# A sandwich layer on one core: couples of heads in the first 120 attention steps, VectorE's bias ahead of its split, and the projection one tile sooner

## The reference

```
x  = x + layernorm(attention(layernorm(x)))
x  = x + layernorm(ffn(layernorm(x)))

attention: xq = rms_norm(x @ wq.T), 32 heads of 64
           xk = rms_norm(x @ wk.T), xv = x @ wv.T, 8 heads of 64 (each serves 4 query heads)
           scores = xq @ xk.T / 8 + slope[h] * (key - query)
                    allowed only for 0 <= query - key <= 256
           out = softmax(scores) @ xv        -> [tokens, 2048]
           return out @ wo.T                 -> [tokens, 512]
```

## Time and profile before

| | us |
|---|---|
| median of three runs | 1213.42 |
| the profiled execution, its own time | 1213.68 |
| its span, first to last instruction | 1211.5 |
| PE busy | 1176.3 |
| DVE busy | 896.9 |
| ACT busy | 749.5 |
| POOL busy | 390.6 |

### The profile page before, as it was taken

The page is one execution under the profiler, slowest core; times in us unless marked ns, Lnnn a source line. Parts: engine busy times, 40 slices in busy tenths (PEclk is TensorE's granted clock), DMA queues, the critical chain, the costliest instruction groups (busy, mean ns, idle before and its releaser), DMA issues.

```text
span 1211.5 us, 26996 instructions
## 1 busy us (share of the span) xinstructions
PE 1176.3 (97%) x9016; PEld 998.2 (82%) x9016; DVE 896.9 (74%) x2388; ACT 749.5 (62%) x1641; POOL 390.6 (32%) x465
## 2 busy tenths in 40 slices
PE   7999999999999999999999999999999999999997
PEld 5878888887877778889898899889888888887876
DVE  5577778687999988888888888888865475546464
ACT  4645556555899888878888788888833343222230
POOL 3000000000689985544545454544421100202022
PEclk9999999999999999999999999999999999999999
DMA  5316355346567777445654556455555340302020
GB/s 174 104 44 232 151 200 216 127 196 252 194 227 238 230 240 239 145 164 167 219 177 152 174 185 214 142 166 168 160 195 173 121 129 35 104 1 88 18 70 36
DMA packets 99876, 189.89 MB, mean 157 GB/s; under 512 B 8096, under 2 KB 37920, under 8 KB 99744
## 3 DMA queue, kind: packets, MB, share of 16 engines
q1 hardware_dynamic: 99744, 188.21, 46.3%
HBM read 116.54 MB, written 71.63 MB: 155 GB/s over the span
## 4 chain that ended last, share of the span: by engine, by line
PE 85%; DVE 4%; ACT 3%; issue 3%; POOL 2%; DMA 2%; SPq 0%; POOLq 0%; ACTq 0%; DVEq 0%
PE bank L1330 21%; PE bank L1477 17%; PE bank L1404 13%; PE bank L1356 12%; PE bank L1367 11%; PE bank L1385 2%; PE bank L1383 2%; PE bank L1384 2%; PE bank L1393 2%; DMA z_in<-z_scr 1%; ACT pT_hi L866 1%; PE bank L1454 1%; POOL y_s L735 1%; PE bank L1298 1%; DVE y_s L989 1%
## 5 line engine op out<-in xcount | busy, mean ns | idle before, releaser
L859 ACT ACTIVATE p_sb<-u_sb,low 128x384 f32<-128x384 f32 (+2 forms) x512 | 274.6, 536 | 57.3 <-DVE low L1105 48.6
L1112 DVE TENSOR_TENSOR pT_lo<-bank,pT_hi 128x384 f16<-128x384 f32 (+2 forms) x512 | 232.4, 454 | 43.7 <-ACT pT_hi L866 32.9
L1356 PE MATMUL bank<-k_st,q_st 128*128 128x384 f32 (+2 forms) x1024 | 255.9, 331 | 2.4 <-DVE low L1105 2.4
L1105 DVE CUSTOM_DVE_ANT_0 u_sb<-bank,bias 128x384 f32<-128x384 f32 (+2 forms) x512 | 230.3, 450 | 34.2 <-PE bank L1356 18.6
L1367 PE MATMUL bank<-ident,p_sb 128*128 128x128 f32 x1152 | 217.9, 280 | 13.9 <-DVE pT_lo L1112 5.8
L866 ACT ACTIVATE pT_hi<-bank 128x384 f16<-128x384 f32 (+2 forms) x512 | 206.8, 404 | 38.9 <-PE bank L1367 34.1
L1356 PEld LDWEIGHTS bank<-k_st,q_st 128*128 128x128 f32 x1024 | 168.3, 192 | 17.6 <-DVE low L1105 2.7
L1367 PEld LDWEIGHTS bank<-ident,p_sb 128*128 128x128 f32 x1152 | 138.6, 140 | 49.4 <-ACT p_sb L859 22.3
L614 POOL TENSOR_TENSOR rstd<-var_eps,minus_half 128x1 f32<-128x1 f32 (+1 forms) x30 | 22.6, 754 | 426.0 <-DVE var_eps L971 426.0
L652 POOL TENSOR_TENSOR o_mid<-o_raw,inv_sum 128x256 f32<-128x256 f32 x128 | 80.9, 632 | 219.4 <-DVE inv_sum L1120 217.9
L1383 PE MATMUL bank<-v_st,pT_hi 128*128 128x65 f16 x1152 | 139.8, 193 | 0.5 <-DVE pT_lo L1112 0.5
(11 more groups left out here) (126 smaller groups left out, 2315.5 us busy)
## 6 DMA issues: line engine op xcount, KB each, us to landing
q_scr<-qk SPq DMA_DIRECT2D x64, 512.0 KB, 2.7
q_st<-q_scr SPq DMA_DIRECT2D x32, 1024.0 KB, 7.6
k_st<-k_scr SPq DMA_DIRECT2D x64, 256.0 KB, 3.2
o_scr<-o_out SPq DMA_DIRECT2D x128, 128.0 KB, 2.5
o_in<-o_scr SPq DMA_DIRECT2D x16, 1024.0 KB, 5.6
k_scr<-qk SPq DMA_DIRECT2D x16, 512.0 KB, 2.7
z_in<-z_scr SPq DMA_DIRECT2D x8, 1024.0 KB, 6.8
v_scr<-v_out SPq DMA_DIRECT2D x4, 1040.0 KB, 6.2
```

The lines of the kernel that those rows point to most:

```text
L859: nc.scalar.activation(p_sb[:, u % RING, 0:w], u_sb[:, u % RING, 0:w], ACT.Exp, scale=-1.0, bias=low[:, u % RING:u % RING + 1]).then_inc(p ...
L1105: nc.vector.tensor_tensor_reduce(out=u_sb[:, u % RING, 0:w], in0=bank[u % 2][:, 0:w], in1=bias[2 * u // UNITS][:, u % REP, at:at + w], sca ...
L1112: nc.vector.tensor_tensor(pT_lo[:, u % RING, 0:w], bank[2 + u % 2][:, 0:w], pT_hi[:, u % RING, 0:w], ALU.subtract).then_inc(pT_ready, 1)
L1356: mm = nc.tensor.matmul(bank[u % 2][:, 0:w], q_st[:, s, r, P * i:P * i + P], k_st[:, s, part, P * key:P * key + w], start=(part == 0), sto ...
```

## The change

1. **Couples.** For the first 120 units (`TWINS`) the stages behind the transpose are done for two neighbouring units at once: `round_pT` and `split_pT` are one ACT and one DVE instruction over two PSUM banks (2,3 or 6,7 in turn). The tables of lags have an entry for even and one for odd units. In a couple (A, A+1) PE transposes in steps A+2 and A+3, ACT rounds in step A+3, DVE splits in step A+5, PE weighs both in step A+6.
2. **VectorE's order.** In those steps DVE does `add_bias` of the step's unit first and the split of a couple second (`DVE_ORDER`).
3. **First scores ahead.** Scores, bias and exponential of units 0 and 1 stand ahead of the last product of the last `project`.
4. **LAG is 4 instead of 5.** The projection is woven in from tile of attention 4 on, and the tail projects tiles 12 to 15. The output weights are loaded and split in tiles 0 to 3 instead of 1 to 4. The loads of the attention outputs are cut in two, three quarters and the last quarter (`tile_last`).
5. **Smaller moves.** Five left-over query parts instead of four in a tile of attention; `sum_squares` of the keys of the first sequence goes behind product 21; the count of low bits is taken inside attention.

```diff
-LAG = TT + 1
+LAG = TT
-LAGS = {"split": 3, "scores": 0, "transpose": 2, "exps": 0, "weigh": 4, "take": 5, "invert_sums": 6}
-COUPLE_LAGS = {**LAGS, "take": 6, "invert_sums": 7}
+LAGS = {"split": (3, 3), "scores": (0, 0), "transpose": (2, 2), "round": (2, 2), "exps": (0, 0),
+        "weigh": (4, 5), "take": (6, 6), "invert_sums": (7, 7)}
+DVE_ORDER = ("transpose", "round", "exps", "weigh", "take", "scores", "split", "invert_sums")
+TWIN_LAGS = {**LAGS, "split": (5, 4), "round": (3, 2), "weigh": (6, 5), "invert_sums": (9, 9)}
+AHEAD = 2
+TWINS = LAG * UNITS - 2 * TT
...
-LATE_UNITS = (2, 4, 18, 20)
+LATE_UNITS = (2, 4, 18, 20, 22)
...
+def probability_bank(unit):
+    return unit % 2 + (6 if unit < TWINS and unit // 2 % 2 else 2)
...
             def round_pT(n, u):
+                A, w, at = UNITS * n + u, P * window(u // REP % TT)[1], u % RING
+                if A >= TWINS:
...
+                elif u % 2:
+                    act.wait_ge(pT_psum, A + 1)
+                    at_least(act, pv_done, A - RING + 1)
+                    nc.scalar.activation(pT_hi[:, at - 1:at + 1, 0:w], pairs[probability_bank(A) // 2][:, :, 0:w],
+                                         ACT.Copy).then_inc(pT_hi_ready, 2)
...
             def split_pT(n, u):
...
+                elif u % 2:
+                    dve.wait_ge(pT_hi_ready, A + 1)
+                    nc.vector.tensor_tensor(pT_lo[:, at - 1:at + 1, 0:w], pairs[probability_bank(A) // 2][:, :, 0:w],
+                                            pT_hi[:, at - 1:at + 1, 0:w], ALU.subtract).then_inc(pT_ready, 2)
...
             def unit_work(n, u):
-                for stage, nn, uu in due(n, u):
+                for stage, nn, uu in sorted(due(n, u), key=lambda d: UNITS * n + u < TWINS and DVE_ORDER.index(d[0])):
...
             def transpose_p(n, u):
-                at_least(pe, pT_ready, A - 1)
+                if A < TWINS:
+                    at_least(pe, pT_ready, A - A % 2 - 2)
+                else:
+                    at_least(pe, pT_ready, A - 1 if A > TWINS + 1 else TWINS - 2)
...
+                    if n == NGEMM - 1 and last:
+                        for u in range(AHEAD):
+                            scores(0, u)
...
-                    if n == QC + KVC:
+                    if n == QC + KVC + first:
                         sum_squares(b, 1)
```

More of the change, by code:

```diff
@@ L139, in due @@
 def due(n, u):
[L142 to L145, removed]
+    step = UNITS * n + u
+    for stage in LAGS:
+        for unit in range(max(0, step - LONGEST), min(step + 1, UNITS * B * TT)):
+            lag = (TWIN_LAGS if unit < TWINS else LAGS)[stage][unit % 2]
+            if stage in ("scores", "exps") and unit < AHEAD:
+                continue
+            if unit + lag == step and (stage not in OF_FOUR_HEADS or unit % REP == REP - 1):
+                yield stage, *divmod(unit, UNITS)
+def probability_bank(unit):
+    return unit % 2 + (6 if unit < TWINS and unit // 2 % 2 else 2)
 def transposed_at(n, u):
@@ L526, in attend @@
                 store_late(n, UNITS // 2, UNITS)
-                for i in range(TT // 2):
-                    store_o(n, 1, i)
+                if n == B * TT - 1:
+                    load_o(tile + 2)
+                store_o(n, 1, 0)
             sp.wait_ge(gemm_done, NGEMM * B)
@@ L534, in _ @@
                 attend(n)
-            for i in range(TT // 2, TT):
+            for i in range(1, TT):
                 store_o(B * TT - 1, 1, i)
+                if i < TT - 1:
+                    load_o(B * TT - LAG + i - 1, last=True)
             def load_z(tile, m, done):
@@ L888, in unit_work @@
                 for stage, nn, uu in due(n, u):
-                    work = {"transpose": round_pT, "exps": exps, "take": take_values}.get(stage)
+                    work = {"round": round_pT, "exps": exps, "take": take_values}.get(stage)
                     if work:
@@ L1075, in project @@
                             split_xT(b + 1)
+                        if n == NGEMM - 1 and last:
+                            for u in range(AHEAD):
+                                add_bias(0, u)
                         dve.wait_ge(v_hi_ready, TT * b + n - QC - KVC + 1)
@@ L1272, in _, with scores @@
             pe.wait_ge(const_ready, CONSTANTS)
+            def scores(n, u):
+                A, s, i, r = UNITS * n + u, 2 * u // UNITS, u // REP % TT, u % REP
+                key, tiles, _ = window(i)
+                w = P * tiles
+                if u % (UNITS // 2) == 0:
+                    pe.wait_ge(heads_loaded[s], 3 * DMA * (n + 1))
+                if n == 0 and u < 2:
+                    pe.wait_ge(v_ready, TT * (B - 1) + u + 1)
+                at_least(pe, u_ready, A - 1)
+                for part in range(2):
+                    mm = nc.tensor.matmul(bank[u % 2][:, 0:w], q_st[:, s, r, P * i:P * i + P],
+                                          k_st[:, s, part, P * key:P * key + w], start=(part == 0), stop=(part == 1))
+                mm.then_inc(s_psum, 1)
             def transpose_x(b):
@@ L1465, in _ @@
             lo_used = pe.value_load(lo_total[:].bitcast(mybir.dt.int32))
-            for t in range(B * TT - TT + 1, B * TT):
+            for t in range(B * TT - LAG + 2, B * TT):
                 finish_tile(t)
```

167 lines of the change are left out of this document (79 added, 88 removed).

## The result

The changed kernel takes 1249.05 us, the median of 4 runs (1245.67 to 1252.54). The kernel before, run beside it, took 1213.35 (1213.11 to 1215.61). The ratio is 1.029 [1.0259, 1.0321]: **slower by 35.7 us**. The prediction said 1245.5 and 1229 to 1263. The profiled execution took 1248.71 us with a span of 1246.5.

A forecast was written before the change was run, and what follows sets the result against it. PE bounds tiles with a projection; in the others PE, DVE, ACT and POOL are nearly full. From the profiled 1213.7 us, + 41.4 - 2 - 5.7 - 1.4 = 1246.0; predicted 1245.5 us, range 1229 to 1263.

The forecast's parts named there:

- loop, 120 units: Attention's first 120 units: scores, bias, couple's split, transpose, weighing, next odd scores form a slackless loop; +41.4 us, 35 to 47.
- clock in the loop: First 120 units: PE was taken to keep the full 2.4 GHz, so the sum held nothing for the clock.
- start of attention: First scores ahead, -2 us (0 to -4), and the `sum_squares` wait behind product 21 covered, -1.4 us.
- tile 4: Tile of attention 4 now carries a projection: 38.84 instead of 31.6 us, +7.2.
- tail: Output projection after attention: one tile less, -12.9 us.
- seven terms: Three-block loop: scores 0.44, hop 0.38, `add_bias` 0.56, split 0.97, hop 0.14, transposes 0.35, weighing 0.54; 3.38 us in all.
- The split over two banks: DVE's split of six blocks in the loop: 0.97 us, bounds 0.82 and 1.11, with no row showing one.
- The clock: Rival: in the loop PE's clock swings, at half clock for half of the 120 units; 27.6 us more, 1273 us; chance 0.08.
- First scores ahead: Start of attention: PE's idle time before the first scores and the half-clock stretch after it shrink; -2 us, 0 to -4.
- LAG: Tile 4 gains a projection, +7.2 us, and the tail loses a tile, -12.9 us; together -5.7 us.
- the rival of the tail's cover: Tail: late loads of the last outputs make PE wait up to some 5 us; 1250.5 us; 0.77 shared with the plain loop.
- The wait does not bind: Rival at PE's transpose (L1411): split done in time, POOL next at about 33 us a tile; 1204.5 us; chance 0.12.

The follow-up runs named there:

- kernel with full clock: Changed kernel with each odd unit's transposes in the first 120 units done three times over; 1242.87 us, ratio 1.0253 to the kernel before.
- the kernel with the sum in even steps: Changed kernel with an added VectorE sum of two SBUF operands behind each even unit's bias, 59 times in the first 120 steps; 1268.23 us.

## Why the prediction was right

It was right in direction, cause and size: 1249.05 measured, 1245.5 predicted, and most of its steps hold one by one. The sum ended 3.5 us low, 2.7 of it in the terms below: one that I had put at nothing was 6 us, and the loop, tile 4 and the tail, each 0.9 to 1.5 us shorter than foretold, hid more than half of that. That the total is so near is in part luck.

| term | predicted | measured | from |
|---|---|---|---|
| loop, 120 units | +41.4 | +39.9 | kernel with full clock: 171.1 less 131.2 for four tiles |
| clock in the loop | 0 | +6.1 | 46.0 less 39.9; the whole run says 6.2 |
| start of attention | -2 and -1.4 | -3.0 | of it the wait of the earlier trace rows -1.4 |
| tile 4 | +7.2 | +6.3 | 37.9 less 31.6 |
| tail | -12.9 | -14.4 | windows |
| tiles 5 to 15 | 0 | +0.1 | starts of `add_bias` |
| sum | +32.3 | +35.0 | span: +35.0 |

*The loop.* Its seven terms were each within 0.02 us but one: the bias. I counted its full duration (0.56); in the trace the split starts 0.48 after it, beside the one-column read. Over the eight turns of half a tile that is 8 x 0.08 = 0.64 us, about the 0.5 by which they came out shorter. The four tiles came out 1.5 us shorter than predicted. The split over two banks, for which I had kept 0.82 to 1.11, was 0.95 against 0.97. Signs foretold and seen: tiles of 42 to 46 us (43.3 to 45.3), DVE under 75% (28.7 / 43.3 = 66%), 60 waits of 1 us (54). The starts 3.4 apart were seen (3.3), but in 2 turns of 16 only. Tile 4, foretold at 38 to 39 us, took 37.9.

*The clock.* Here the step "In this trace it was granted the full 2.4 GHz in all tiles with short waits ... That speaks for full clock" failed. Those tiles had PE busy 30.0 of 32.6 us; nothing in them spoke for a tile in which PE is busy 27.8 of 43.3. Three times beside the one at the start the clock fell to 1.2 GHz, at 319, 408 and 452 us. Ahead of them PE was busy 3.8, 3.7 and 3.7 of 6.8 us; in the first two it was busy 6.2 of 6.8. PE is on the loop for about 1.3 of 3.29 us (scores, transposes, weighing), so a slower PE is paid at once. The Trainium skill, page "TensorE: Matmul & The Clock Gate", section "A second HAM failure mode: psum-queue depth-cycling", describes a clock that swings when PE idles briefly between groups of matmuls. By that rule the trace agrees, in part: one tile of four (336.8 to 380.1, clock 1.00) shows the same small gaps, in its like part with the same 3.7 us of PE in 6.8, and no fall. Why it was spared these rows don't tell. The sign that I had named for the clock, tiles over 48 us, could not have shown a cost of this size. I had given this rival 0.08 and 27.6 us, for half of the units; 6 us is what it took. A rival can be half true, and its price belongs into the sum by its chance or at least into the middle of the range.

*First scores ahead.* -2 predicted, -1.6 measured beyond the `sum_squares` wait. That one is gone as foretold: PE waits nowhere at L1350.

*LAG.* Tile and tail together: -8.1 instead of -5.7. The tail is shorter by one tile and by the 1.0 us of waits for `oT_lo`; no load stood bare, so the rival of the tail's cover did not come.

*The wait does not bind.* It does. But this rival was rightly built: with the loop opened, POOL was next as it said, at 34.8 us a tile where it said 33, and the kernel came to 1208.0 where it said 1204.5.

*What no run isolated.* Whether the order costs anything with single units, since every run without couples also had the split first. And what the 5.5 us between couples and singles are made of, both with the split first: the couples save 161 ns of DVE in a three-block couple (2 x 0.557 less 0.953), but they also have four banks instead of two and other lags.

## What to carry to other kernels

- Before moving one operation ahead of another on an engine, write down what each waits for and go round: if the second one's result is what the first one's producer stands behind, the two now alternate and nothing else matters. The sum of the terms round that loop, from rows of the trace, was right to 3% here.
- An order is not slow as such: couples with the split first took 1208.0 us, couples with the bias first and the split a step sooner 1210.0, and only bias first with the late split 1249.0. Move one step or one place in the order before dropping an edit, and look in the trace whether the run undid just what you meant: a condition on the number of units tied the order to the couples here.
- When a loop or wait goes, look for the engine that is next, and take load off it in the same step: with the split first, the kernel with POOL's fifth part gained 5 us on the one before, without it 11.

## What the runs showed of the hardware

**A slower PE by idling, a faster one by useless work.** The odd transposes done three times gave back 6.2 of 1249 us, and the runs agree to 1 us instead of 7. The clock read 0.99 over the four tiles instead of 0.88 to 1.00.

**A DVE sum of two SBUF operands stands still while POOL works.** In the kernel with the sum in even steps, 34 of 59 took 0.56 us on average. The other 25 began while POOL was in a tensor-tensor instruction (or within 0.06 us of its start) and took 1.34 on average, up to 2.88; in 23 of them the end came 0.41 us after POOL's instruction ended, as at 356.13 + 2.75 = 358.88 and 356.83 + 2.46 = 359.29. The bias and the split, each with one operand in PSUM, took 0.55 and 0.95 whatever POOL did. The Trainium skill, page "SBUF — State Buffer", section "SBUF: two separate sides", says that a VectorE operation with two SBUF inputs and a GpSimd operation that reads SBUF take turns whole, the one that starts first going first. The trace agrees. A probe meant to cost a known time must not have two SBUF operands beside a working POOL.

**DVE instructions overlap by some 0.08 us.** A bias of 0.56 us is followed 0.48 us later, a three-block sum of 0.56 by the next at 0.47, a two-block one of 0.42 at 0.34. A sum over DVE instructions in a row goes by starts; the last one alone counts with its full duration.
